# Recurrent heads of a thirteen-layer kernel: all four products of the float16 parts, and inputs and mixing in one-pass products of 128 columns

## Time and profile before

| | |
|---|---|
| median of three runs | 3305.01 us |
| the profiled execution | 3309.41 us, its span 3307.7 us |
| TensorE busy over the span | 2969.3 us (90%) |
| VectorE, ScalarE, GpSimd busy | 2120.6, 1626.9, 1099.5 us |
| granted TensorE clock over the span | 0.88 |
| the layer's loop | 829 to 1404 us |

### The profile page before, as it was taken

The page is one execution under the profiler, slowest core; times in us unless marked ns, Lnnn a source line. Parts: engine busy times, 40 slices in busy tenths (PEclk is TensorE's granted clock), DMA queues, the critical chain, the costliest instruction groups (busy, mean ns, idle before and its releaser), DMA issues. The chain is left out here.

```text
span 3307.7 us, 56895 instructions
## 1 busy us (share of the span) xinstructions
PE 2969.3 (90%) x21826; PEld 1723.4 (52%) x21833; DVE 2120.6 (64%) x4817; ACT 1626.9 (49%) x3321; POOL 1099.5 (33%) x587
## 2 busy tenths in 40 slices
PE   7888899999899999998987898897889889989998
PEld 3333344443888888843434444444454344564547
DVE  6777634545555555556569877777781549935991
ACT  3555432523333333334356777676763557734762
POOL 1111100000100000000048878788770208931990
PEclk8999999999555555599998989998999899999999
DMA  5443332032000000011243222222210201250224
GB/s 153 102 100 91 82 115 80 1 93 76 3 3 3 3 3 3 3 59 47 75 165 96 91 78 83 89 87 82 82 57 0 100 0 64 89 203 1 89 92 189
DMA packets 113486, 234.22 MB, mean 71 GB/s; under 512 B 13760, under 2 KB 50752, under 8 KB 104768
## 3 DMA queue, kind: packets, MB, share of 16 engines
q1 hardware_dynamic: 113216, 230.59, 21.6%
HBM read 185.71 MB, written 44.83 MB: 70 GB/s over the span
## 5 line engine op out<-in xcount | busy, mean ns | idle before, releaser
L2507 DVE TENSOR_TENSOR_SCAN s_hh<-psum,s_dbu 128x512 f32<-128x512 f32 x384 | 447.6, 1208 | 76.5 <-ACT psum L2119 75.3
L2377 POOL TENSOR_TENSOR s_dbu<-s_du,s_bb 128x1024 f32<-128x1024 f32 x191 | 446.8, 2360 | 66.5 <-DVE s_hh L2507 56.7
L1249 PE MATMUL psum<-h_now,h_parts 128*128 128x4 f16 x12264 | 415.5, 168 | 54.9 <-DVE h_now L1374 54.9
L1249 PEld LDWEIGHTS psum<-h_now,h_parts 128*128 128x128 f16 x12264 | 408.4, 106 | 92.5 <-DVE h_now L1374 76.4
L1321 ACT ACTIVATE h_hist<-psum 128x16 f32<-128x16 f32 x1024 | 188.6, 184 | 388.7 <-PE psum L1249 317.3
L1374 DVE TENSOR_SCALAR h_now<-h_hist 128x16 f16<-128x16 f32 x1022 | 188.8, 185 | 208.2 <-ACT h_hist L1321 208.2
L2119 ACT ACTIVATE psum<-s_delta,s_decay 128x512 f32<-128x512 f32 x384 | 256.6, 686 | 112.0 <-DVE s_hh L2507 109.8
L1333 POOL TENSOR_TENSOR h_lay<-w_c,h_xt 128x128 f32<-128x128 f32 x128 | 50.1, 412 | 676.2 <-PE psum L1239 497.8
L2011 PEld LDWEIGHTS psum<-w_c,s_term 128*128 128x128 f32 x1536 | 202.8, 152 | 136.3 <-issue 116.1
L911 DVE TENSOR_TENSOR f_hid<-f_gate,psum 128x512 f32<-128x512 f32 x184 | 126.5, 687 | 204.8 <-PE psum L837 197.8
L898 ACT ACTIVATE f_gate<-psum 128x512 f32<-128x512 f32 x184 | 109.7, 597 | 281.6 <-PE psum L833 281.5
(11 more groups left out here) (527 smaller groups left out, 5996.8 us busy)
## 6 DMA issues: line engine op xcount, KB each, us to landing
s_bb<-s_wide SPq DMA_DIRECT2D x192, 256.0 KB, 3.5
x_spill<-x_flip SPq DMA_DIRECT2D x28, 1024.0 KB, 3.8
f_share<-f_wide SPq DMA_DIRECT2D x208, 128.0 KB, 3.0
s_cc<-s_wide SPq DMA_DIRECT2D x60, 256.0 KB, 3.3
a_ks<-a_spread SPq DMA_DIRECT2D x96, 128.0 KB, 3.3
a_qs<-a_spread SPq DMA_DIRECT2D x96, 128.0 KB, 3.9
x_spare<-x_spill SPq DMA_DIRECT2D x4, 2048.0 KB, 7.7
x_raw<-x_spill SPq DMA_DIRECT2D x4, 2048.0 KB, 7.8
```

The lines of the kernel that those rows point to most:

```text
L1249: mm = nc.tensor.matmul(here[:, cols], parts[:, part, GROUP * grp + p, :], now[:, grp, cut, cols], start=False, stop=True, skip_group_chec ...
L2377: nc.gpsimd.tensor_tensor(dbu[:, s % D_RING], du[:, t % 2], both(bb[:, s % B_RING, :]), ALU.mult).then_inc(dbu_ready, 1)
L2507: nc.vector.tensor_tensor_scan(hh[:, s % 4, half, :], DECAYS[i % 3], dbu[:, s % D_RING, half, :], 0.0, ALU.mult, ALU.add).then_inc(scan_do ...
```

```diff
-    PAIRS, S, BLOCK = 8, 64, 8
+    PAIRS, BLOCK = 8, 32
-    BLOCKS, SPAN, PIECE = TIME // BLOCK, 128, 32
-    RAISED = 2.0 ** 15
-    LAY_AT = (1, 3)
-    MIX_AT = tuple(s for s in range(PIECE) if s % BLOCK in (5, 7))
+    BLOCKS, SPAN, RING = TIME // BLOCK, 128, 64
+    RAISED, X_RAISED = 2.0 ** 15, 2.0 ** 12
+    PRODUCTS = ((0, 0), (0, 1), (1, 0), (1, 1), (2, 0))
+    ITEMS = PAIRS * len(PRODUCTS)
...
-                def lay_inputs(blk, grp):
-                    pe.wait_ge(laid, blk + 1)
-                    nc.tensor.matmul(columns_of(blk, grp), w["b"], lay[:, blk % 2, grp, :, :],
-                                     start=True, stop=True).then_inc(laid_free, 1)
+                def input_item(blk, n):
+                    p, (part, cut) = n // len(PRODUCTS), PRODUCTS[n % len(PRODUCTS)]
+                    if n == 0:
+                        pe.wait_ge(x_split, blk + 1)
+                    mm = nc.tensor.matmul(columns_of(blk, p // GROUP)[:, :, p % GROUP * BATCH:(p % GROUP + 1) * BATCH],
+                                          b_parts[:, part, p, :], x_parts[:, cut, blk * BLOCK:(blk + 1) * BLOCK, :],
+                                          start=(n % (ITEMS // 2) == 0), stop=True, skip_group_check=True)
+                    if n == ITEMS - 1:
+                        mm.then_inc(laid, 1)
+                def mix_item(blk, n):
+                    p, (part, cut) = n // len(PRODUCTS), PRODUCTS[n % len(PRODUCTS)]
+                    if n == 0 and blk == 0:
+                        pe.wait_ge(c_split, 1)
+                    grp, col, per = p // GROUP, p % GROUP * BATCH, SPAN // BLOCK
+                    first_slot = blk * BLOCK % RING
+                    mm = nc.tensor.matmul(bank[4 + blk // per][:, blk % per * BLOCK * BATCH:(blk % per + 1) * BLOCK * BATCH],
+                                          c_parts[:, part, p * P:(p + 1) * P], ring[:, first_slot:first_slot + BLOCK, grp, cut, col:col + BATCH],
+                                          start=(n == 0), stop=(n == ITEMS - 1), skip_group_check=True)
...
                     pe.wait_ge(rest[grp], i)
+                    product(1, 1)
                     product(0, 1).then_inc(drive[grp], 1)
...
-                    if s in LAY_AT and blk + 1 < BLOCKS:
-                        lay_inputs(blk + 1, LAY_AT.index(s))
-                    if piece and place in MIX_AT:
-                        mix_in(piece - 1, MIX_AT.index(place))
+                    for n in range(ITEMS * s // BLOCK, ITEMS * (s + 1) // BLOCK):
+                        if blk + 1 < BLOCKS:
+                            input_item(blk + 1, n)
+                        if blk:
+                            mix_item(blk - 1, n)
                 warm(nc, g, bank[0], 4)
                 for grp in range(2):
-                    pe.wait_ge(state[grp], TIME)
-                for n in range(PAIRS):
-                    mix_in(TIME // PIECE - 1, n)
+                    pe.wait_ge(rest[grp], TIME)
+                for n in range(ITEMS):
+                    mix_item(BLOCKS - 1, n)
...
-                act.wait_ge(x_ready, CHUNKS)
-                act.wait_ge(laid_free, 2)
+                act.wait_ge(laid, 1)
...
-                        nc.scalar.activation(hist[:, i, grp, :], columns_of(blk, grp)[:, s, :], ACT.Tanh,
+                        nc.scalar.activation(now[:, grp, :], columns_of(blk, grp)[:, s, :], ACT.Tanh,
...
-                pool.wait_ge(x_ready, CHUNKS)
-                for blk in range(BLOCKS):
-                    put(blk)
+                nc.gpsimd.tensor_scalar(w["b"], w["b"], w["norm_w"], RAISED * RAISED / X_RAISED, ALU.mult, ALU.mult).then_inc(b_raised, 1)
...
+                for k in range(3):
+                    done = nc.gpsimd.tensor_tensor(b_parts[:, k], b_cut[:, k, :].unsqueeze(1).broadcast_to([P, PAIRS, P]),
+                                                   g.pair_of[:, 0:PAIRS].unsqueeze(2).broadcast_to([P, PAIRS, P]), ALU.mult)
+                done.then_inc(b_spread, 1)
+                def cut_inputs(blk):
+                    steps = slice(blk * BLOCK, (blk + 1) * BLOCK)
+                    nc.gpsimd.tensor_copy(x_parts[:, 0, steps, :], xt[:, steps, :]).then_inc(x1_kept, 1)
+                    pool.wait_ge(x1_kept, blk + 1)
+                    nc.gpsimd.tensor_tensor(x_parts[:, 1, steps, :], xt[:, steps, :], x_parts[:, 0, steps, :], ALU.subtract).then_inc(x_split, 1)
+                pool.wait_ge(x_split, 1)
+                cut_inputs(1)
+                nc.gpsimd.tensor_copy(c_parts[:, 0, :], w["c"]).then_inc(c1_kept, 1)
+                pool.wait_ge(c1_kept, 1)
+                nc.gpsimd.tensor_tensor(c_left[:, :], w["c"], c_parts[:, 0, :], ALU.subtract).then_inc(c_rest, 1)
...
+                for blk in range(2, BLOCKS):
+                    cut_inputs(blk)
...
-                for i in range(TIME - 1):
+                for i in range(TIME):
                     for grp in range(2):
                         dve.wait_ge(state[grp], i + 1)
-                        nc.vector.tensor_scalar(now[:, grp, 0, :], hist[:, i, grp, :], RAISED, None, ALU.mult).then_inc(first[grp], 1)
+                        nc.vector.tensor_scalar(ring[:, i % RING, grp, 0, :], now[:, grp, :], RAISED, None, ALU.mult).then_inc(first[grp], 1)
```

More of the change, by code:

```diff
@@ L1207, in recurrent_heads @@
         xt = sb("h_xt", [P, TIME, BATCH])
-        lay = sb("h_lay", [P, 2, 2, BLOCK, WIDTH])
-        now = sb("h_now", [P, 2, 2, WIDTH], F16)
-        hist = sb("h_hist", [P, TIME, 2, WIDTH])
+        x_parts = sb("h_xparts", [P, 2, TIME, BATCH], F16)
+        now = sb("h_now", [P, 2, WIDTH])
+        ring = sb("h_ring", [P, RING, 2, 2, WIDTH], F16)
         mix = sb("h_mix", [P, BATCH, TIME])
-        early = hist[:].rearrange("p t g c -> p (t g c)").rearrange("p (k j c) -> p k j c", j=CHUNKS, c=CHUNK)
+        early = sb("h_early", [P, 2, CHUNKS, CHUNK])
         norm = InnerNorm(g, sems[:6], bank[0:4], bank[4:6], early[:, 0], early[:, 1])
         def columns_of(blk, grp):
-            return bank[2 * (blk % 2) + grp][:, 0:BLOCK * WIDTH].rearrange("p (s c) -> p s c", c=WIDTH)
+            return bank[2 * (blk % 2) + grp].rearrange("p (s c) -> p s c", c=WIDTH)
         with nc.Block() as block:
@@ L1248, in product @@
                             cols = slice(BATCH * p, BATCH * p + BATCH)
-                            mm = nc.tensor.matmul(here[:, cols], parts[:, part, GROUP * grp + p, :], now[:, grp, cut, cols],
+                            mm = nc.tensor.matmul(here[:, cols], parts[:, part, GROUP * grp + p, :], ring[:, (i - 1) % RING, grp, cut, cols],
                                                   start=False, stop=True, skip_group_check=True)
@@ L1256, in advance @@
                     pe.wait_ge(rest[grp], i)
+                    product(1, 1)
                     product(0, 1).then_inc(drive[grp], 1)
[L1259 to L1271, removed]
+                pe.wait_ge(b_spread, 1)
+                for n in range(ITEMS):
+                    input_item(0, n)
                 pe.wait_ge(a_split, 1)
@@ L1274, in _ @@
                     blk, s = divmod(i, BLOCK)
-                    piece, place = divmod(i, PIECE)
                     for grp in range(2):
@@ L1325, in _ @@
             def _(pool):
[L1326 to L1337, removed]
@@ L1343, in _ @@
+                pool.wait_ge(c_rest2, 1)
+                nc.gpsimd.tensor_copy(c_parts[:, 2, :], c_left[:, :]).then_inc(c_split, 1)
+                for blk in range(2, BLOCKS):
+                    cut_inputs(blk)
+                nc.gpsimd.tensor_scalar(w["out"], w["out"], 1.0 / RAISED, None, ALU.mult).then_inc(scaled, 1)
             @block.vector
@@ L1369, in _ @@
                     scale(j)
-                for i in range(TIME - 1):
+                dve.wait_ge(x_ready, CHUNKS)
+                nc.vector.tensor_copy(x_parts[:, 0, 0:BLOCK, :], xt[:, 0:BLOCK, :]).then_inc(x1_kept, 1)
+                dve.wait_ge(x1_kept, 1)
+                nc.vector.tensor_tensor(x_parts[:, 1, 0:BLOCK, :], xt[:, 0:BLOCK, :], x_parts[:, 0, 0:BLOCK, :], ALU.subtract).then_inc(x_split, 1)
+                for i in range(TIME):
                     for grp in range(2):
                         dve.wait_ge(state[grp], i + 1)
-                        nc.vector.tensor_scalar(now[:, grp, 0, :], hist[:, i, grp, :], RAISED, None, ALU.mult).then_inc(first[grp], 1)
+                        nc.vector.tensor_scalar(ring[:, i % RING, grp, 0, :], now[:, grp, :], RAISED, None, ALU.mult).then_inc(first[grp], 1)
                         dve.wait_ge(first[grp], i + 1)
-                        nc.vector.scalar_tensor_tensor(out=now[:, grp, 1, :], in0=hist[:, i, grp, :], scalar=RAISED, in1=now[:, grp, 0, :],
-                                                       op0=ALU.mult, op1=ALU.subtract).then_inc(rest[grp], 1)
+                        nc.vector.scalar_tensor_tensor(out=ring[:, i % RING, grp, 1, :], in0=now[:, grp, :], scalar=RAISED,
```

(1 more changed line is left out.)

45 lines of the change are left out of this document (35 added, 10 removed).

## The result

| | before | changed |
|---|---|---|
| median, 20 runs each | 3304.2 us | 3311.05 us |
| lowest to highest | 3299.3 to 3310.8 | 3305.9 to 3315.4 |
| ratio, with its 95% interval | | 1.0020 (1.0013 to 1.0027) |
| the profiled execution, its span | 3309.4, 3307.7 us | 3311.6, 3309.9 us |

What follows compares the result with a forecast made beforehand. The recurrent loop was taken as bound by a latency chain in plain steps and TensorE in float32 steps, after the change by TensorE throughout; loop +9.0, head +3.9, tail +1 gave +13.9, so 3319 us, range 3303 to 3350.

Steps and rivals of the forecast that it cites:

- E in part 3 of the change: In the loop's steps, the time the first small product loses behind the wide ones: 0.02 us taken, bounds 0 and 0.05.
- TensorE is the bound in every step: In the loop, TensorE needs 1.087 us (two wide products) or 1.300 (four), both just over the chain's 1.074.
- The fourth product, + 0.107 on the chain: `product(1, 1)`, four more small products per group and step: 4 x 0.0267 = 0.107 us, plain step from 0.97 to 1.074.
- A wide product at 0.107, its weights hidden: Each one-pass, 128-column product for inputs or mixing costs TensorE 0.107 us if its weights load behind the product ahead.
- open-weights rival: Wide products' weights load in the open: 0.027 us more each, 3350 us; 0.13 shared with another price of mixed types.
- two-pass rival: Wide products take two passes after all, 0.213 us each, steps of 1.30 and 1.73 us: 3446 us; chance 0.03.
- GpSimd, + 5: At the loop's head, GpSimd's cutting of mixing weights holds VectorE's cuts: 5 us, a quarter of 20, bounds 1 and 15.
- Head, + 3.9: Before the loop, the first tanh waits for all 40 wide products and VectorE cuts the first inputs: 3.9 us more.
- Tail, + 1: After the loop, the last mixing's 40 products take 4.3 us against 3.24, part at full clock: 1 us more.
- The clock stays at half: TensorE's granted clock stays 0.50 in the loop; the rival that it rises gave 3248 us, chance 0.06.
- All bounds low: Rival: E = 0, GpSimd 1 us, head +1, tail 0, loop and head -1 in all: 3304 us; chance 0.16.

## Why the forecast had the right sign and was twice too large

- **The step that failed: E in part 3 of the change**, what the first small product behind a run of wide ones loses. I gave it 0.02 us in each step, beside 0.107 for each wide product, from what the same instruction loses after an idle wait; no row had a wide 16-bit product ahead of a small one. In sum it is 0. With 0.02, steps of 1.087 and 1.300 were forecast and 1.073 and 1.280 came: 336 x 0.014 + 112 x 0.020 = 7 us, the loop's whole miss. The first small product does lose 0.04 behind four wide ones, but the first wide product is followed after 0.06 instead of 0.107 us, which gives it back: I had priced only the tail of the run. A price for a run must be taken from a start before it to a start well behind it.
- **Which limit decides.** "TensorE is the bound in every step" was wrong in three steps of four, by those 0.02: its need is 1.067 in steps with two wide products, the chain's 1.073. The runs with the fourth product taken out and with four combinations show the chain; the run with doubled mixing and the bursts show TensorE.
- **The sign.** It rests on small terms. With E = 0 and all else as it stood, the forecast's own sum is 571.8 + 5 - 574.6 = +2.2 for the loop and +7.1 in all. That this is close to the 6.9 of the medians is in part luck: the stage itself shows 4.8, chiefly as the tail came out 1.4 lower. The loop's small difference is what is left of two large ones, -65.5 and +67.
- **The fourth product, + 0.107 on the chain:** right. 0.967 to 1.073 us in the new kernel, 0.966 to 1.075 in the one before.
- **A wide product at 0.107, its weights hidden:** right, by the doubled mixing. bf16 weights with float16 data cost one pass. The open-weights rival and the two-pass rival fall: with 0.027 more for each, the step with three wide products would have taken 1.253 us, and it took 1.173. So the rule that I quoted from the Trainium skill (TensorE: Matmul & The Clock Gate, Part 3, The mechanism) doesn't hold for these products, which use all rows.
- **GpSimd, + 5:** 4.5, by what the first 32 steps lose. The first block takes 38.85 us where 32 steps of 1.074 are 34.4. But it isn't a quarter of 20 us of small collisions, as I had argued: 3.0 of it are two steps in which a cut waits for the end of a long operation. The size was right by luck, the mechanism half right. Both cuts can be held, the second too: 344 and 333 ns at most in the earlier trace rows. The Trainium skill (GPSIMD Engine Reference, 1. Specifications) names this contention for VectorE instructions in a 2-port mode or with two SBUF inputs; that the second cut, with two inputs, is held agrees, and which mode the first one runs in no run shows.
- **Head, + 3.9:** +3.6. **Tail, + 1:** -0.4. The forty products took 3.06 us against 3.24 for the sixteen float32 ones. The granted clock was 0.50 from 1410 to 1411 us and 1.00 from 1412 to 1413; the forecast's +1 is what forty at half clock would have cost.
- **The clock stays at half:** right, but for the loop's first 3 us: it went to full while the forty products ahead of the loop followed each other without a gap.
- "All bounds low", 0.16, was close to what the loop did (-1.8 against +1.6), for its E = 0 and in spite of its GpSimd of 1 us; the head kept the kernel on the slower side.

## What to carry to other kernels

In a loop whose steps hang on each other, work beside the chain is free only up to the pause of its own step; cut it into pieces that fit there before making it cheaper. Here that made most of 61 us, and the same pieces in bursts cost 75; each product added on the chain cost its slot in nearly every step. When two limits lie within 1% of each other, the price of one instruction must be measured where only one of them acts, for example by doubling the work beside the chain.

## What was unexpected of the hardware

- A VectorE operation of 175 ns took 2.10 us when GpSimd had just begun a long one. It ended 0.04 us behind GpSimd's end. Here long GpSimd operations beside a chain on VectorE cost by their length more than by their share of the time.
- At half clock the first of four wide products was followed after 0.06 us and the others after 0.10 to 0.12; the difference comes back behind the run.
- TensorE's idle time can be nothing in a trace while it pauses: in the run without the fourth product it is busy for 400.00 of 400 us, though three steps in four end with a pause of 0.11 us (0.967 less 0.853).
